# Moving the x1T and q splits in a plan by steps, and making x1 on ScalarE instead of VectorE

## What is computed

```python
q, k, v = jnp.split(x @ Wqkv + bqkv, 3, axis=2)       # q, k centred, squared, normalised
kv = jnp.einsum('bnc,bnd->bcd', k2, v)
y  = x + (v + einsum('bnc,bcd->bnd', q2, kv) / sqrt(N)) @ Wln + bln
x1 = layernorm(y)
sel = sigmoid(einsum('bsd,ed->bse', x1, expert_sel))
z  = x1 + einsum(relu(x1 @ keys), values, sel)
out = layernorm(z)
```

## Time and profile before

| | |
|---|---|
| median of 3 runs | 1062.44 us (1060.86 to 1063.06) |
| profiled execution, its own time | 1055.52 us |
| its span, first to last instruction | 1053.7 us |
| mean granted TensorE clock | 0.984 of 2.4 GHz |
| busy: PE, DVE, ACT, POOL | 95%, 79%, 47%, 20% |

### The profile page before, as it was taken

How to read it: one execution, slowest core, us unless ns; L and a number is a source line. 1 busy time by engine, 2 the same in 40 slices (tenths; PEclk the granted TensorE clock), 3 DMA queues, 4 the chain that set the end, 5 groups by cost and what they waited for, 6 DMA issues and landing times.

```text
span 1053.7 us, 21920 instructions
## 1 busy us (share of the span) xinstructions
PE 1003.5 (95%) x8324; PEld 988.1 (94%) x8324; DVE 828.2 (79%) x1874; ACT 495.1 (47%) x1090; POOL 212.3 (20%) x267
## 2 busy tenths in 40 slices
PE   8999998999989999899989999899998999989997
PEld 7899998999989999899989999899998999989996
DVE  5889886889768988698876988779886889758554
ACT  4556633465335653356524564336543466333332
POOL 0021212212122122221212111222121222212221
PEclk9999999999999999999999999999999999989999
DMA  5041112111122121121111211112111211110100
GB/s 178 22 143 39 43 61 81 55 49 62 42 82 81 41 70 39 56 101 42 62 40 53 91 42 61 42 62 81 43 61 42 80 62 42 61 42 22 42 21 21
DMA packets 47981, 62.19 MB, mean 59 GB/s; under 512 B 4098, under 2 KB 34562, under 8 KB 47876
## 3 DMA queue, kind: packets, MB, share of 16 engines
q1 hardware_dynamic: 47876, 60.79, 17.0%
HBM read 37.18 MB, written 23.07 MB: 57 GB/s over the span
## 4 chain that ended last, share of the span: by engine, by line
PE 78%; DVE 11%; issue 4%; DMA 4%; ACT 1%; SPq 1%; DVEq 0%; POOL 0%; ACTq 0%; POOLq 0%
PE down_bank L1315 27%; PE up_bank L1315 27%; PE ring_bank L1315 9%; PE qk_bank L1315 7%; PE g_bank L1315 3%; DMA z<-parked_x 2%; DMA parked_x<-w_room 2%; DVE gated_l L1085 1%; SPq L445 1%; PE ring_bank L1566 1%; DVE gated L1079 1%; DVE x1T_l L944 1%; DVE z L981 1%; PE ring_bank L1567 1%; DVE k_total L1010 1%
## 5 line engine op out<-in xcount | busy, mean ns | idle before, releaser
L553 ACT ACTIVATE gated_h<-gated 128x512 fp32r<-128x512 f32 x256 | 161.9, 632 | 393.0 <-DVE gated L1079 392.9
L539 POOL PARTITION_BROADCAST sel_all<-sel_rows x240 | 197.7, 824 | 716.8 <-DVE gated L1079 684.5
L1315 PE MATMUL down_bank<-vals_h,gated_h 128*128 128x256 f32 x1024 | 291.1, 284 | 12.4 <-DVE z L981 10.9
L1315 PE MATMUL down_bank<-vals_l,gated_h 128*128 128x256 f32 x1024 | 287.6, 281 | 0.0
L1315 PE MATMUL down_bank<-vals_h,gated_l 128*128 128x256 f32 x1024 | 287.5, 281 | 0.0
L1315 PE MATMUL up_bank<-x1T_h,keys_h 128*128 128x256 f32 x1024 | 286.0, 279 | 0.0
L1315 PE MATMUL up_bank<-x1T_l,keys_h 128*128 128x256 f32 x1024 | 285.8, 279 | 0.0
L1315 PE MATMUL up_bank<-x1T_h,keys_l 128*128 128x256 f32 x1024 | 285.6, 279 | 0.0
L1079 DVE SCALAR_TENSOR_TENSOR gated<-up_bank,sel_all 128x512 f32<-128x512 f32 x256 | 176.2, 688 | 49.0 <-PE up_bank L1315 46.9
L1085 DVE TENSOR_TENSOR gated_l<-gated,gated_h 128x512 fp32r<-128x512 f32 x256 | 171.8, 671 | 52.4 <-ACT gated_h L553 51.7
L1315 PEld LDWEIGHTS down_bank<-vals_h,gated_h 128*128 128x128 f32 x1024 | 196.1, 191 | 17.6 <-issue 13.7
(11 more groups left out here) (250 smaller groups left out, 1677.4 us busy)
## 6 DMA issues: line engine op xcount, KB each, us to landing
out<-z SPq DMA_DIRECT2D x32, 256.0 KB, 2.4
x_raw<-in_x SPq DMA_DIRECT2D x15, 512.0 KB, 4.7
xT_raw<-in_xT SPq DMA_DIRECT2D x14, 512.0 KB, 4.0
parked_q<-w_room SPq DMA_DIRECT2D x14, 512.0 KB, 2.6
q<-parked_q SPq DMA_DIRECT2D x56, 128.0 KB, 3.0
parked_x<-w_room SPq DMA_DIRECT2D x14, 512.0 KB, 2.6
z<-parked_x SPq DMA_DIRECT2D x56, 128.0 KB, 2.9
w_room<-in_keys SPq DMA_DIRECT2D x4, 512.0 KB, 4.3
```

Source lines behind the costliest of these rows:

```text
L539: nc.gpsimd.partition_broadcast(sel_all[:, e % 2], row, P).then_inc(sel_spread, 1)
L553: return nc.scalar.activation(dst, src, ACT.Copy, **kw)
L1315: last = mm(dst, lhs, rhs, start=start and i == 0, stop=stop and i == n - 1, **kw)
```

## The change

The diff shows the plan, `bias_x`, a new function of ScalarE (called from its `early` for every Y of the step before), `finish_ys` and `add_zs` of VectorE. It moves entries of the plan: the q tiles 4 to 7 are transposed in steps 16, 18, 19 and 20 (before 15 to 18), QR 0 goes from 16 to 20, XR 0 from 28 to 29, LG 0 from 29 to 30, and the bias of the last x pair from 30 to 28. And x1 of all tiles that the loop makes (60 of 64) is made on ScalarE as `y * rstd + shift`; VectorE makes the shift, one value a row, in its place.

```diff
-        15: [("GG", 4), ("QK", 6), ("QS", 4)],
-        16: [("QR", 0), ("GG", 5), ("QS", 5)], 17: [("ZA", 0), ("ZA", 1), ("QK", 7), ("QS", 6)],
-        18: [("GG", 6), ("QS", 7)], 19: [("KS", 0), ("ZN", 0), ("GG", 7)],
-        20: [("ZN", 1)], 21: [("KV", 0)], ...
-        25: [("Y", 3), ("XS", 2)], 26: [("XS", 3)], 27: [("QR", 1)], 28: [("XR", 0)], 29: [("LG", 0)],
+        15: [("GG", 4), ("QK", 6)],
+        16: [("GG", 5), ("QS", 4)], 17: [("ZA", 0), ("ZA", 1), ("QK", 7)],
+        18: [("GG", 6), ("QS", 5)], 19: [("KS", 0), ("ZN", 0), ("GG", 7), ("QS", 6)],
+        20: [("QR", 0), ("ZN", 1), ("QS", 7)], 21: [("KV", 0)], ...
+        25: [("Y", 3), ("XS", 2)], 26: [("XS", 3)], 27: [("QR", 1)], 29: [("XR", 0)], 30: [("LG", 0)],
...
-    bias_x={9: 0, 14: 1, 27: 2, 30: 3},
+    bias_x={9: 0, 14: 1, 27: 2, 28: 3},
...
+            def x1_normalised(b, a): 
+                act.wait_ge(y_shift_made, tile(b, a) - GT)
+                if b == 1:
+                    act.wait_ge(x1_transposed, tile(0, a))
+                if b > 0:
+                    act.wait_ge(z_added, 2 * (G * (b - 1) + a // GT) + (a % GT) // 2 + 1)
+                nc.scalar.activation(x1[:, a], y[:, a % 2], ACT.Identity, bias=y_shift[:, a % 2:a % 2 + 1],
+                                     scale=y_rstd[:, a % 2:a % 2 + 1]).then_inc(x1_made, 1)
...
                 for _, a, off in ys: 
                     dve.wait_ge(y_inverted, tile(it + off, a))
-                    if it + off == 1:
-                        dve.wait_ge(x1_transposed, tile(0, a))
-                    elif it + off > 1:
-                        dve.wait_ge(staged, GT * park(it + off - 1, "XS", a // GT) + a % GT + 1)
-                    layer_norm(x1[:, a], y[:, a % 2], y_mv[:, a % 2],
-                               y_rstd[:, a % 2:a % 2 + 1]).then_inc(x1_made, 1)
+                    V.scalar_tensor_tensor(out=y_shift[:, a % 2:a % 2 + 1], in0=y_mv[:, a % 2, 0:1], scalar=-1.0,
+                                           in1=y_rstd[:, a % 2:a % 2 + 1], op0=ALU.mult, op1=ALU.mult
+                                           ).then_inc(y_shift_made, 1)
...
                     at_least(dve, stored[a], it * (16 * G) + off * 16) 
                     if 0 < it < B:
                         dve.wait_ge(x1T_lo, tile(it, T - 1) if off == 0 else tile(it, GT - 1))
+                    dve.wait_ge(x1_made, tile(it + (off - off % G) // G, t + 1))
```

More of the change, by code:

```diff
@@ L167, in build_program @@
         y_stats, y_mv = sb("y_stats", [P, 2, 6]), sb("y_mv", [P, 2, 2])
-        y_std, y_rstd = sb("y_std", [P, 2]), sb("y_rstd", [P, 2])
+        y_std, y_rstd, y_shift = (sb(n, [P, 2]) for n in ("y_std", "y_rstd", "y_shift"))
         z_stats, z_mv = sb("z_stats", [P, 2, 2, 6]), sb("z_mv", [P, 2, 2, 2])
@@ L247, in build_program @@
         staged, parked, landed_q, landed_x = map(sem, ("staged", "parked", "landed_q", "landed_x"))
-        y_joined = sem("y_joined")
+        y_joined, y_shift_made = sem("y_joined"), sem("y_shift_made")
         q_transposed, qT_hi, qT_lo = map(sem, ("q_transposed", "qT_hi", "qT_lo"))
@@ L602, in k_normalised_hi @@
                                      scale=k_scale[:, t % 2:t % 2 + 1]).then_inc(k_fourth, 1)
+            def x1_normalised(b, a):
[6 more added lines that the diff above has]
+                                     scale=y_rstd[:, a % 2:a % 2 + 1]).then_inc(x1_made, 1)
             def early(it, s):
-                for kind, t, off in planned(it, s - 1, ("QK", "KS", "LG")):
-                    if kind == "LG":
+                for kind, t, off in planned(it, s - 1, ("QK", "KS", "LG", "Y")):
+                    if kind == "Y":
+                        x1_normalised(it + off, t)
+                    elif kind == "LG":
                         act.wait_ge(logits_summed, half(it + off, t))
```

## The result

The changed kernel takes 1027.54 us (median of 4 runs, 1025.22 to 1028.49) against 1062.75 us before (4 runs, 1060.86 to 1064.42): a ratio of 0.9666, 95% interval 0.9643 to 0.9689, 35.2 us faster. The profiled execution took 1027.94 us, its span 1026.1 us, so between the two profiled executions only 27.6 us lie.

A forecast was written before the change was run, and what follows sets the result against it. PE, busy for 95% of the span, was taken as the floor, with only its pauses to win. -24.3 - 11.3 + 5.6 = -30.0 us gave 1025.5 profiled, 1032.5 us with the 6.9 us distance; range 1024 to 1047.

The forecast's parts named there:

- Logits: XR 0 to step 29, LG 0 to 30: 22.6 us of pauses and 10.5 of low clock go, 8.8 come, -24.3 us.
- The q tiles: Step 17's wait for z goes, -11.3 us; QR 0 in step 20 makes kvw_l 0.8 us late, 5.6 us in seven.
- x1 on ScalarE: 60 x1 moved from VectorE to ScalarE: zero gain and zero cost, bounds 0 to 0.6 us a tile.
- Bias: Bias moved into step 28 delays gated(28) by 0.6 us: a new pause of 0.8 us before down(28).
- sel and SP: Rows of `sel` for the next half, fetched through SP and memory, broadcast from step 0: cost nothing, cover 2 us.
- the first rival: Clock stays low at the boundaries, two close pauses taken as one: 10.5 us back, 1043 us, chance 0.14.
- 5 x 1.7 + 2.0 = 10.5 us: PE time lost to the lower clock after the logits pauses: five boundaries at 1.7 us, the last 2.0.
- I keep that distance: Median of runs, 1062.4 us, lies 6.9 above the profiled 1055.5; the same was added to 1025.5, giving 1032.5 us.
- The rival of the carried wait: Logits wait only carried along, x1's transfer also a step later on SP's queue: 1062.5 us, no change, chance 0.03.
- that of ScalarE's queue: x1 holds up gated_h in every Y step by 0.59 us: 35.3 us on top of -30.0, 1067.7 us, chance 0.05.

The follow-up runs named there:

- the logits alone: Kernel before with only XR 0 moved to step 29 and LG 0 to step 30, bias left at 30: 1033.65 us, ratio 0.975.
- x1 twice: Changed kernel with ScalarE making each x1 twice, the first into a tile nobody reads: 1029.42 us, 0.8 us above the changed kernel.
- x1 on ScalarE alone: Kernel before with all of the diff but the plan and `bias_x`: 1060.32 us over 12 runs, ratio 0.9996.
- q alone: Kernel before with only QS 4 to 7 moved to steps 16, 18, 19, 20 and QR 0 to 20: 1054.66 us, ratio 0.9931.
- before again: Kernel before, unchanged, measured once more: 1060.62 us over 12 runs, ratio 1.0003.
- after again: Changed kernel, unchanged, measured once more in the second job: 1028.61 us over 6 runs, 0.9694 of the kernel before.
- bias in 30: Changed kernel with the bias of the last x pair back in step 30: 1023.76 us, 0.9645 of the kernel before.
- QR 0 in 18: Changed kernel with QR 0 in step 18 in place of 20: 1025.63 us, 3.0 us below the changed kernel.
- both repairs: Changed kernel with the last x pair's bias back in step 30 and QR 0 in step 18: 1021.97 us, 0.9642 of the kernel before.
- bias in 29: Changed kernel with the bias of the last x pair in step 29 in place of 28: 1026.4 us, 0.9672 of the kernel before.
- XR 0 in 28: Changed kernel with XR 0 back in step 28 and LG 0 staying in 30: 1037.34 us, ratio 0.9785.

## Why the prediction was right, and where it was short

**The mechanism** held: the waits that were to go went, the ones that were to come came, at the places named.
- *Logits.* Forecast: 22.6 us of pauses go, 8.8 us of two short pauses come. Measured: the pauses 22.6 to 4.3, the new one at down(28) 4.3, so 8.6 us. That the sum fits so well is partly luck: the pause at down(28) was put at 0.8 us and is 0.5 to 0.7, the one at the logits at 0.45 and is 0.6. Alone, without the bias, 27.1 us.
- *The q tiles.* Forecast -11.3 + 5.6. The trace: 11.3 to 1.5, and 4.6 for kvw_l, in sum -5.2; timed alone -6.1. I had put the rest in step 17 at nothing, and it is 0.3 us in five iterations; the KV pause at 0.8 us, and it is 0.65.
- *x1 on ScalarE.* Forecast nothing. Alone 0.4 us, within the noise; doubled, 0.8 us. The 0.3 us of cover behind that forecast were not there, but what lay behind them, 1 us at PE, was enough.
- *Bias.* Costed at 0.8 us a boundary. Taking it out gives 4.9 us, 0.7 us a boundary, in step 30; in 29 about half of that.
- *sel and SP.* Costed at nothing, with 2 us of cover. In step 0 of the sixth iteration POOL's first broadcast of the fetched rows starts at 674.59 and its gate, in step 1, at 679.04.
- *The clock* does not fall at short pauses, so the first rival fell as well: 1.00 in all windows shown, and 0.993 to 0.999 as the mean of the changed kernel's ten executions. None of the nine profiles with LG 0 in step 30 has a low clock anywhere between the first 53 us and the last 8.

**The size was short by 5 us**: 30.0 forecast, 35.2 measured between the medians of the first comparison, 32.4 in the second. Between the two profiled executions it is the other way round, 27.6 measured. The pauses are not the reason: those in the forecast's sum come to 19.5 us (22.6 + 11.3 - 8.8 - 5.6) and measured 19.2. Two other terms were off.
- *"5 x 1.7 + 2.0 = 10.5 us" of low clock.* The low stretch at the last boundary was read only to the edge of its window; with the rest the term is 5 x 1.7 + 3.4 = 11.9 us in this very profile. And the profile was of an execution with less low clock than most. Over 57 further executions of the kernel before the mean clock is 0.982 in the middle (0.977 to 0.988), so at most 19.1 us lost in 1059 in place of 16.9; over ten of the changed kernel it is 0.995, 5.1 us. By this estimate the clock is worth 14 us between typical executions. With the 19.7 us by which the pauses of the table shrank that is 34 us, between the two measurements.
- *"I keep that distance."* The 6.9 us between profile and median before did not carry over: afterwards they are -0.4 us. The profiled execution of the kernel before was an unusually quick one, only one of the 57 was quicker (1052.86 us). Its clock accounts for some 2 us of the 6.9 (19.1 less 16.9); where the other 5 lie stays open. Without this distance the forecast would have been 1025.5 us, 2 us from the measured 1027.5 in place of 5.

The pauses repeat closely but not exactly: at the logits they are 22.6 us by the starts in the first profile and 24.1 in the second one of the same kernel.

**The rival of the carried wait** is out by the logits alone, that of ScalarE's queue by x1 twice, where the second x1 puts the copy half a microsecond late in the Y step shown and PE does not wait. The Trainium skill's advice against adds and multiplies on ScalarE ("ScalarE: Activation LUTs", section "Rules for kernel authors") is right as to the price, 601 against 413 ns in these rows, and says nothing of a kernel in which neither engine is waited for in that place.

## What to carry to other kernels

When one engine is busy for 95% of the span, look at its few pauses, one by one, and at what the clock does behind them: moving an entry by one step was worth 27 us. Of what the whole change gave, some two fifths was clock, by the estimate above. A step in which a hand-written plan holds nothing is not wholly free if it lies on the chain of the engine that is waited for; carry that chain on by hand from the last point that the bottleneck did not wait for, over at least three steps. And take the distance between a profiled execution and the median as noise, above all when what is removed is the thing that varies.

## What the hardware showed that I had not expected

**The low clock is not always the same.** The logits pauses of the kernel before were of 2.8 to 3.6 us by the starts, and after the one of 2.8 us at 300 us no lower clock followed; in the profile of x1 on ScalarE alone three of the seven (3.0, 3.1 and 3.7 us) were followed by none, and with q alone one of 2.8 us. So the length of the pause alone doesn't decide. The shortest that had a lower clock behind it was 2.9 us. Repeated, the same kernel's mean clock goes from 0.977 to 0.988. No pause up to 1.7 us was followed by a lower clock in the loop, in thirteen profiles; between 1.7 and 2.8 us there was none to look at. (The Trainium skill, "TensorE: Matmul & The Clock Gate", section "What's actually happening", says that TensorE is throttled by default and that activity releases the throttle. The trace agrees in so far as the lower clock came in the loop only at the long pauses.)

**TensorE has two paces at full clock.** Twelve matmuls of 256 columns take 1.36 or 1.41 us, 0.1133 or 0.1177 us each, for tens of microseconds on end, at a granted clock of 1.00. Which one holds changes mostly at a pause or at an attention product. Over a profile, counted in groups of twelve by the spacing of their starts:

```
                      mean spacing ns   matmuls in slower groups / in faster
before                      115.3            3352 / 4432
after                       115.4            3467 / 4417
before again                115.2            3140 / 4645
logits alone                115.7            4089 / 3808
q alone                     115.7            4040 / 3763
x1 on ScalarE alone         115.9            4484 / 3337
after again                 115.4            3447 / 4453
bias in 30                  115.2            3152 / 4740
QR 0 in 18                  115.8            4327 / 3601
x1 twice                    115.2            3048 / 4817
both repairs                115.5            3681 / 4217
bias in 29                  115.4            3520 / 4394
XR 0 in 28                  116.3            5163 / 2733
```

One nanosecond in the mean is 8 us over some 8,000 matmuls. So pace can hide or feign a difference of a few us between two profiled executions. It may be a part of what XR 0 in 28 lost beyond its pauses, but that is not shown: its profiled execution was the slowest of the six (1041.59 us against a median of 1037.34), and the pace of the others is not known. In the profile the pace is seen as the number of matmuls in a window in which PE never stops; here are two such windows of the changed kernel's profile in the second job, PE alone, at a clock of 1.00. The first holds four logits matmuls of 512 columns, each of which takes two places (0.23 us), so 172 places stand against 179:

```profile
592.00:612.00 20.00, 20.00 (x168) 1.00 0.16 54
720.00:740.00 20.00, 20.00 (x179) 1.00 0.17 56
```

What sets the pace was not found. It is each time one profiled execution, and I have no run that changes the pace and nothing else.
